# Choice of the experts' tokens rewritten: ranks in 128 partitions, a threshold without bit masks, the list from two sets of one-hot columns, all in one block

## The chip, the core and the metric

The kernel runs on one core of one Trainium2 chip. A core has a matrix engine (TensorE, "PE" in the profile, with "PEld" for its weight loads), three engines for elementwise work (VectorE "DVE", ScalarE "ACT", GpSimd "POOL") and a queue engine (SyncE, "SP") that issues most DMA transfers. The engines run on their own and meet through semaphores. The metric is the device time of one launch in microseconds (us), lower is better.

## What is computed

Eight stages act on `x` of shape (8, 512, 256), that is 4096 tokens of 256 numbers: four cross attentions, and four feed-forward parts between them. The change lies inside one of these, the expert-choice layer. Its reference, cut to what matters here:

```python
scores = jax.nn.sigmoid(h @ gate_w.T)               # h: (4096, 256), 16 experts
cap = math.ceil(T / E * TOP_K)                      # 4096 / 16 * 2 = 512
topk_score, topk_ids = jax.lax.top_k(scores.T, cap) # each expert picks its 512 best tokens
xin = h[topk_ids]
...                                                 # expert MLP on 512 x 256, per expert
flat = (eo * topk_score[..., None]).reshape(-1, Dm)
out = jnp.zeros_like(h).at[topk_ids.reshape(-1)].add(flat)
```

The order within `topk_ids` does not matter for the sum. The kernel needs the 512 token numbers of each of the 16 experts in a tile `index` of 128 partitions x 16 experts x 4, which later indirect DMAs read as lists of rows to fetch and to add to.

## The kernel before, in words

`P` is 128, `S` 512, `CE` 16 (experts), `CAP` 512, `NT` 32 (tiles of 128 tokens), `SB` and `TB` 4. `expert_choice` calls three parts one after the other: `shared_expert` writes the scores of all tokens to `l1f_scoresT` (16 x 4096) in DRAM, `choose_tokens` turns them into `index`, and `run_experts` loads the weights, gathers rows and computes. Between the parts all engines meet at barriers: a `nc.Block()` ends only when every engine is at its end, and `stage_semaphores` clears semaphores and has one more barrier. No weights of the experts are loaded ahead, so nothing of the other two parts lies beside the choice.

`choose_tokens` has five blocks before the change.

1. Set-up. SP loads the scores twice: as `s128` (each expert's row cut in 8 chunks of 512, chunk c of expert e in partition 16 c + e; eight transfers, L2910) and as `s16` (16 partitions x 4096, L2911). GpSimd and VectorE make constants, among them `same`, a 128 x 128 matrix that is 1 where two partitions belong to the same expert.
2. Threshold (L2943 to L2968). The score of rank 512 of each expert is found two bits at a time in 15 rounds of a hardware loop (`Fori`). In a round VectorE forms four candidates from the threshold so far, counts in three passes how many scores reach them (L2950, with a sum along the row), TensorE adds the counts over the 8 chunks of an expert with `same` (two matmuls, L2967 and L2968), and VectorE turns the sums into two bits by masks and exclusive-ors (L2955 to L2960). `chained` gives each dependent instruction a semaphore wait on the one before.
3. Ranks (L2975 to L3006). On `s16`, in 16 partitions of 4096 columns: which scores lie above the threshold, which equal it and still have room, a running count (the scan) as the rank of each chosen token, and from it a slot 0 to 511, with values past 511 for tokens not chosen. TensorE turns this to tokens in partitions (32 transposes, L3006), VectorE cuts the slot in slot / 4 (`slot_p`) and slot modulo 4 (`slot_j`), and makes `numbers`: for each of 4 values of `slot_j`, the token's partition and its tile where it matches, else 0 (L2993 to L2998).
4. List (L3013 to L3029). For each of 32 tiles VectorE builds a one-hot matrix of `slot_p` over 128 values for 16 experts (L3020, 2048 columns), and TensorE multiplies it, expert by expert, with that tile's 8 columns of `numbers` (16 matmuls, L3029), all added up in `psI`.
5. Two instructions make token = 128 x tile + partition and write `index` (L3036, L3038).

The order of everything is as written in the code, engine by engine.

Of the kernel before, what the change touches and what calls it, by code (L numbers as in the profile page):

```python
# [2869 lines left out]
def choose_tokens(nc, A, G, sT_dram, index):  # L2870
# [7 lines left out]
    BITS = 30  # L2878
    with ExitStack() as ctx:
        sb = lambda n, s, d=F32: ctx.enter_context(nc.sbuf_tensor("ch_" + n, s, d))  # L2880
# [3 lines left out]
        same_i, same = sb("same_i", [P, P], I32), sb("same", [P, P])  # L2884
        thr = sb("thr", [P, 1], I32)

        tries, bits, cand, keep = (sb(n, [P, 4], I32) for n in ("tries", "bits", "cand", "keep"))
        count = sb("count", [P, 4])
        s16, above, equal, rank = (sb(n, [CE, N_TOK]) for n in ("s16", "above", "equal", "rank"))
        n_above, room = sb("n_above", [CE, 1]), sb("room", [CE, 1])  # L2890
        slot = sb("slot", [P, NT, CE], I32)
        slot_i = sb("slot_i", [P, NT, CE], I32)
        slot_p, slot_j = sb("slot_p", [P, NT, CE], BF16), sb("slot_j", [P, NT, CE], BF16)
        iota_i, iota_p, iota_j = sb("iota_i", [P, P], I32), sb("iota_p", [P, P], BF16), sb("iota_j", [P, SB], BF16)
        part_i, part_f = sb("part_i", [P, 1], I32), sb("part_f", [P, 1])
        tile_f = sb("tile_f", [P, NT])
        hot_p = sb("hot_p", [P, 2, CE, P], BF16)
        hot_j, numbers = sb("hot_j", [P, NT * CE, SB]), sb("numbers", [P, NT, CE, 2 * SB], BF16)
        zeros = sb("zeros", [P, P], BF16)
        token = sb("token", [P, CE, SB])  # L2900
        psC, psS, psI = psum("psC", [P, S]), psum("psS", [P, NT, CE]), psum("psI", [P, CE, 2 * SB])
        loaded, iotas, set_up, chain = sem("loaded"), sem("iotas"), sem("set_up"), sem("chain")
        counted, summed = sem("counted"), sem("summed")
        slot_ready, slotT_ready, hot_ready, hot_used, index_ready = (sem(n) for n in ("slot_ready", "slotT_ready", "hot_ready", "hot_used", "index_ready"))
# [487 lines left out]
```

## Time and profile before

| | us |
|---|---|
| median of 3 runs | 4851.79 (4846.97 to 4854.86) |
| profiled execution, its own time | 4852.99 |
| span of its trace | 4851.3 |
| TensorE busy in the span | 3982.6 (82%) |
| VectorE busy in the span | 3191.5 (66%) |
| mean granted TensorE clock, as a share of 2.4 GHz | 0.889 |

The span runs from the first to the last instruction of the profiled execution; the rest of its own time lies around it. Busy shares are means over eight very different stages. The view by stretches gives, for each interval of the span, how long each engine was busy and which clock TensorE was granted; the view in order of time lists instructions with start and duration, and in square brackets how long the engine was idle before and what released it. The view by line adds up instructions of one line. A matmul of 4-byte numbers shows as two, since it takes two passes.

### The profile page before, as it was taken

Reading aid. Unit: us, or ns where it says so; the run is one execution under the profiler, and the core shown is the slowest. Engines: PE = TensorE matmul, PEld = TensorE weight load, DVE = VectorE, ACT = ScalarE, POOL = GpSimd, SP = SyncE. Lnnn points to the kernel's source line nnn. Section 1 sums busy time; section 2 is a strip of 40 time slices with the busy share of each in tenths; the row PEclk is TensorE's granted clock in tenths of the full one; section 3 lists DMA queues with packets and bytes.
Section 4 is the critical chain, followed back from the end, with each engine's and each line's share of the span. In section 5 each row is a group of like instructions: output and inputs, shape, how many; then the busy total and the mean of one; then the engine's idle time right before and its main releaser. Section 6 shows DMA issues by size and latency. Waiting matters only on the chain. (4 is left out here: it accounts for less than half of the span.)

```text
span 4851.3 us, 84441 instructions
## 1 busy us (share of the span) xinstructions
PE 3982.6 (82%) x30868; PEld 2871.1 (59%) x30962; DVE 3191.5 (66%) x7093; ACT 2059.9 (42%) x3636; POOL 790.5 (16%) x508
## 2 busy tenths in 40 slices
PE   6599997888467999785389999549997986799899
PEld 5244443777365777674268888425555665355577
DVE  6466664435565666544866666549985885898587
ACT  2255554233112433342034545217775762577611
POOL 4333321301251000000013332310000011100000
PEclk9799998699767999897579999769998998799999
DMA  6333331101220000010034444532210005122100
GB/s 206 108 96 97 99 87 53 64 18 37 94 86 28 17 17 22 27 43 30 0 118 123 129 124 131 164 102 67 67 52 18 1 25 175 57 66 66 38 14 22
DMA packets 202232, 338.12 MB, mean 70 GB/s; under 512 B 25380, under 2 KB 119125, under 8 KB 201910
## 3 DMA queue, kind: packets, MB, share of 16 engines
q1 hardware_dynamic: 186040, 306.81, 19.8%
q0 software_dynamic: 15888, 27.23, 2.7%
q8 instruction: 195, 3.19, 0.3%
q14 instruction: 109, 0.89, 0.1%
HBM read 242.65 MB, written 106.97 MB: 72 GB/s over the span
## 5 line engine op out<-in xcount | busy, mean ns | idle before, releaser
L1900 ACT ACTIVATE a_pT<-a_psS 128x512 f32<-128x512 f32 x1536 | 835.9, 598 | 397.8 <-PE a_psS L1786 392.6
L1972 DVE TENSOR_REDUCE a_mx<-a_psA 128x1 f32<-128x512 f32 x1024 | 656.6, 685 | 82.8 <-PE a_psA L1764 82.8
L1764 PE MATMUL a_psA<-a_ks,a_qs 48*128 48x512 f32 (+1 forms) x1536 | 403.3, 520 | 159.9 <-PEq L46 94.2
L1801 PE MATMUL a_psZ<-a_pT,a_V 128*17 128x128 f32 x12288 | 487.1, 277 | 0.0
L1968 DVE CUSTOM_DVE_ANT_0 a_scored<-a_psA,a_hide_q 128x512 bf16<-128x512 f32 x512 | 332.6, 688 | 190.3 <-PE a_psA L1764 189.2
L1801 PEld LDWEIGHTS a_psZ<-a_pT,a_V 128*17 128x17 f32 x12288 | 272.2, 97 | 270.5 <-issue 160.0
L1764 PEld LDWEIGHTS a_psA<-a_ks,a_qs 48*128 48x128 f32 (+1 forms) x1536 | 150.9, 191 | 405.8 <-issue 174.9
L1786 PE MATMUL a_psS<-a_qs,a_ks 50*128 50x512 f32 (+1 forms) x1536 | 317.4, 406 | 2.7 <-ACT a_pT L1900 0.8
L3264 DVE SCALAR_TENSOR_TENSOR ex_h<-ex_psU,ex_ub,ex_sg 128x512 f32<-128x512 f32 x129 | 96.9, 751 | 188.5 <-PE ex_psU L159 167.5
L1984 POOL TENSOR_TENSOR X<-X,a_osb 128x512 f32<-128x512 f32 x48 | 61.2, 1280 | 938.1 <-ACT a_osb L1887 920.2
L3210 ACT CAST ex_w_h<-X 128x1024 fp32r<-128x1024 f32 x102 | 106.1, 1040 | 231.1 <-DMA X<-in_L_ffn_gw 227.3
L3131 POOL DMA_INDIRECT ex_xg<-l1f_rows,ex_idx_get x72 | 76.4, 1061 | 591.7 <-DVEq L3295 358.6
L3219 ACT ACTIVATE ex_sg<-ex_psG,ex_gb 128x512 f32<-128x512 f32 x129 | 88.8, 688 | 178.6 <-PE ex_psG L159 177.2
L1786 PEld LDWEIGHTS a_psS<-a_qs,a_ks 50*128 50x128 f32 (+1 forms) x1536 | 148.8, 189 | 19.1 <-ACT a_pT L1900 13.1
L1774 PE MATMUL a_psS<-a_hide_k,identb 128*128 128x512 bf16 x418 | 133.8, 383 | 27.7 <-ACT a_pT L1900 15.7
L987 DVE TENSOR_TENSOR m_early_l<-m_ps,m_early_h 128x512 fp32r<-128x512 f32 x70 | 48.4, 692 | 147.5 <-ACT m_early_h L863 147.5
L157 PE MATMUL ex_psY<-ex_w_h,ex_h_h 128*128 128x256 f32 x512 | 144.2, 282 | 0.1
L157 PE MATMUL l1a_psF<-l1a_win_h,l1a_zh 128*128 128x512 f32 x288 | 121.3, 421 | 27.7 <-DVE l1a_zl L2598 14.3
L159 PE MATMUL ex_psY<-ex_w_h,ex_h_l 128*128 128x256 f32 x512 | 143.7, 281 | 0.0
L158 PE MATMUL ex_psY<-ex_w_l,ex_h_h 128*128 128x256 f32 x512 | 143.6, 280 | 0.0
L1144 PE MATMUL p_psY<-p_w,p_h 128*128 128x256 f32 x512 | 132.9, 395 | 12.0 <-ACT p_h L1221 12.0
L1488 POOL TENSOR_TENSOR a_p_cT_l<-a_p_cT,a_p_cT_h 128x1024 fp32r<-128x1024 f32 x24 | 58.0, 2416 | 494.3 <-ACT a_p_cT_h L1455 493.9
(606 smaller groups left out, 10491.9 us busy)
## 6 DMA issues: line engine op xcount, KB each, us to landing
a_k_parts<-a_p_kp SPq DMA_DIRECT2D x96, 256.0 KB
a_q_parts<-a_p_qp SPq DMA_DIRECT2D x96, 256.0 KB
a_qs<-a_q_parts SPq DMA_DIRECT2D x192, 128.0 KB
a_ks<-a_k_parts SPq DMA_DIRECT2D x192, 128.0 KB
X<-in_L_ffn_gw SPq DMA_DIRECT2D x36, 512.0 KB, 3.7
X<-in_L_ffn_up_w SPq DMA_DIRECT2D x36, 512.0 KB, 3.3
X<-in_L_ffn_down_w SPq DMA_DIRECT2D x36, 512.0 KB, 3.9
top_rows<-blank_rows SPq DMA_DIRECT2D x32, 514.0 KB, 11.4
```

Source lines behind the costliest of these rows:

```text
L157: nc.tensor.matmul(out, wh, xh, start=start and n == 0, stop=False, **kw)
L158: nc.tensor.matmul(out, wh, xl, start=False, stop=False, **kw)
L159: last = nc.tensor.matmul(out, wl, xh, start=False, stop=stop and n == len(pairs) - 1, **kw)
L1144: last = nc.tensor.matmul(out, h[:, m % 2, t * P:(t + 1) * P], w2[:, m, :], start=False, stop=(m == MF - 1), skip_group_check=True)
L1764: nc.tensor.matmul(psA[:, unit(a, par) % 3], qs[r, g % ring, p % 2, q * P:(q + 1) * P], ks[r, g % ring, p % 2], start=True, stop=True).the ...
L1774: nc.tensor.matmul(psS[:, unit(t, par) % 3], G.identb[:], hide_k[:, u % 2, kt, :], start=True, stop=False, skip_group_check=True)
L1786: nc.tensor.matmul(psS[:, unit(t, par) % 3], ks[r, g % ring, p % 2, kt * P:(kt + 1) * P], qs[r, g % ring, p % 2], start=(hidden is None), ...
L1801: last = nc.tensor.matmul(psZ[q * VP:q * VP + VW, g % 2, j * P:(j + 1) * P], V[:, b, kt, g % NG * GH + j, :], pT[:, p % 2, par, kt, q * P: ...
L1900: nc.scalar.activation(pT[:, p % 2, par, kt, :], psS[:, unit(t, par) % 3], ACT.Exp).then_inc(exp_done, 1)
L1968: nc.vector.tensor_tensor_reduce(out=scored[:, par], in0=psA[:, unit(a, par) % 3], in1=hide_q[:, b % 2, q, :], scale=1.0, scalar=HIDDEN, o ...
L1972: nc.vector.tensor_reduce(mx[:, p // 2 % 2, par, p % 2, q:q + 1], psA[:, unit(a, par) % 3], AX_X, ALU.max).then_inc(a_used, 1)
L3210: nc.scalar.copy(w_h[:, s, c, :], whole[:, c, :]).then_inc(w_high, 1)
```

## The change

Everything is in `choose_tokens`; the function's interface, `index` and the order of slots in it stay as they were.

- One block in place of five, with no barrier between its parts. `s16` is no longer loaded. SP issues the eight loads, then waits for the end of the work on the tokens.
- Threshold: the 15 rounds are written out in place of a loop. Three candidates, one matmul (L2999 of the changed kernel). Since the number of candidates that are reached, 0 to 3, is just the value of the two bits, VectorE sums the three comparisons (L2952, `passed`), multiplies by the bits' place value and ors that in. The shift of `tries` comes before the wait for TensorE.
- Ranks: on `s128`, 128 partitions x 512 columns. As an expert now lies in 8 partitions, two small products with `same` and `earlier` (1 where a partition has the same expert and an earlier chunk) carry the counts from chunk to chunk (L3001, L3002, L3004). Four 128 x 128 transposes in place of 32 of 16 x 128.
- List: the slot is cut into slot / 16 (32 values, `slot_a`) and slot modulo 16 (16 values, `slot_j`). VectorE writes 16 columns with the token's partition and 16 with its tile (`numbers`, L2979 and L2980, 128 x 512 each) and 32 one-hot columns (`hot_a`, L2982, 128 x 512 each). TensorE takes four experts at a time: 32 values x 4 experts as 128 weight columns and 32 x 4 moving columns, for 32 tiles and 4 groups of experts, 128 matmuls (L3014). Both operands step through SBUF: neighbouring weight columns lie 256 bytes apart, and the moving ones 256 or 1024 bytes. Of the product only the blocks in which both experts are the same are used.
- Tokens: four blocks of 32 partitions each (L2988, L2991), then a transfer to a DRAM tensor `ch_list` and one back that brings them into the layout of `index` (L2911, L2913 of the changed kernel).

The diff, without most of the removed lines, which stand in the listing above; a line that is only "..." marks what is left out:

```diff
@@ -2876,167 +2876,143 @@
+    AW, JW, GROUPED = 32, CAP // 32, 4
     with ExitStack() as ctx:
+        list_dram = nc.dram_tensor("ch_list", [P * CE * SB], I32).ap()
...
+        hot_a, numbers = sb("hot_a", [P, GROUPED, AW, NT * GROUPED], BF16), sb("numbers", [P, 2, JW, NT * CE], BF16)
+        token = sb("token", [P, SB, GROUPED, SB], I32)
+        psC, psS, psI = psum("psC", [P, S]), psum("psS", [P, TB, P]), psum("psI", [P, GROUPED, 2 * JW * GROUPED])
...
                 chunks = sT_dram.rearrange("e (c s) -> c e s", s=S)
                 for c in range(CHUNKS):
                     sp.dma_start(s128[c * CE:(c + 1) * CE, :], chunks[c]).then_inc(loaded, 16)
-                sp.dma_start(s16[:], sT_dram).then_inc(loaded, 16)
-                sp.wait_ge(loaded, 16 * (CHUNKS + 1))
+                sp.wait_ge(token_ready, GROUPED)
+                sp.dma_start(list_dram.rearrange("(p r) -> p r", p=P), token[:].rearrange("p q g j -> p (q g j)")).then_inc(stored, 16)
+                sp.wait_ge(stored, 16)
+                sp.dma_start(index[:].bitcast(I32).rearrange("p (i g) j -> p i (g j)", i=GROUPED),
+                             list_dram.rearrange("(i p r) -> p i r", p=P, i=GROUPED)).then_inc(fetched, 16)
+                sp.wait_ge(fetched, 16)
+                sp.wait_ge(loaded, 16 * CHUNKS)
...
+                nc.gpsimd.iota(offset_i[:], [[-1, P]], base=P, channel_multiplier=1).then_inc(iotas, 1)
+                nc.gpsimd.iota(row_i[:], [[0, 1]], base=0, channel_multiplier=1).then_inc(iotas, 1)
+                nc.gpsimd.iota(tile_i[:], [[0, GROUPED], [1, NT], [0, GROUPED]], base=0, channel_multiplier=0).then_inc(iotas, 1)
...
+                dve.wait_ge(iotas, 4)
                 link(nc.vector.tensor_scalar(same_i[:], same_i[:], CE - 1, None, ALU.bitwise_and))
+                nc.vector.tensor_scalar(ahead[:], offset_i[:], float(P), None, ALU.is_lt)
+                nc.vector.tensor_copy(tile_b[:], tile_i[:])
+                nc.vector.tensor_copy(row_f[:], row_i[:])
                 link(nc.vector.tensor_scalar(same[:], same_i[:], 0.0, None, ALU.is_equal))
+                nc.vector.tensor_tensor(earlier[:], same[:], ahead[:], ALU.mult).then_inc(consts_set, 1)
...
+                dve.wait_ge(consts_set, 1)
+                dve.wait_ge(loaded, 16 * CHUNKS)
+                for i in range(BITS // 2):
+                    if i > 0:
+                        dve.wait_ge(tried, i)
+                    link(nc.vector.tensor_tensor(cand[:], tries[:], thr[:].to_broadcast([P, 3]), ALU.bitwise_or))
                     for n in range(3):
                         last = nc.vector.tensor_scalar(reached[:, n], s128[:], cand[:, n:n + 1].bitcast(F32), 0.0, ALU.is_ge, ALU.add,
                                                        accum_out=count[:, n:n + 1])
                     last.then_inc(counted, 1)
+                    nc.vector.tensor_scalar(tries[:], tries[:], 2, None, ALU.logical_shift_right).then_inc(tried, 1)
                     dve.wait_ge(summed, i + 1)
 
-                    link(nc.vector.scalar_tensor_tensor(keep[:], psC[:, 0:4], float(CAP), bits[:], ALU.is_ge, ALU.mult))
-                    nc.vector.tensor_scalar(bits[:], bits[:], 2, None, ALU.logical_shift_right)
-                    link(nc.vector.tensor_tensor(keep[:, 0:2], keep[:, 0:2], keep[:, 2:4], ALU.bitwise_xor))
-                    link(nc.vector.tensor_tensor(keep[:, 0:1], keep[:, 0:1], keep[:, 1:2], ALU.bitwise_xor))
-                    nc.vector.tensor_tensor(thr[:], thr[:], keep[:, 0:1], ALU.bitwise_or)
-                    link(nc.vector.tensor_scalar(tries[:], tries[:], 2, None, ALU.logical_shift_right))
+                    link(nc.vector.tensor_scalar(reaches[:], psC[:, 0:3], float(CAP), 0.0, ALU.is_ge, ALU.add, accum_out=passed[:]))
+                    link(nc.vector.tensor_scalar(brought[:], passed[:], float(1 << (BITS - 2 - 2 * i)), None, ALU.mult))
+                    link(nc.vector.tensor_tensor(thr[:], thr[:], brought[:], ALU.bitwise_or))
+
+                t = thr[:].bitcast(F32)
+                nc.vector.tensor_scalar(above[:], s128[:], t, 0.0, ALU.is_gt, ALU.add, accum_out=n_above[:])
+                link(nc.vector.tensor_scalar(equal[:], s128[:], t, None, ALU.is_equal))
+                nc.vector.tensor_tensor_scan(rank[:], equal[:], equal[:], 0.0, ALU.add, ALU.max).then_inc(above_counted, 1)
+                dve.wait_ge(room_summed, 1)
+                link(nc.vector.tensor_scalar(room[:], psC[:, 3:4], -1.0, float(CAP), ALU.mult, ALU.add))
+                link(nc.vector.scalar_tensor_tensor(equal[:], rank[:], room[:], equal[:], ALU.is_le, ALU.mult))
+                link(nc.vector.tensor_tensor(above[:], above[:], equal[:], ALU.add))
+                nc.vector.tensor_tensor_scan(rank[:], above[:], above[:], 0.0, ALU.add, ALU.max).then_inc(rank_counted, 1)
+                dve.wait_ge(rank_summed, 1)
+                link(nc.vector.tensor_scalar(shift[:], psC[:, 4:5], 2.0 * CAP, None, ALU.subtract))
+                nc.vector.scalar_tensor_tensor(rank[:], rank[:], shift[:], above[:], ALU.add, ALU.mult).then_inc(slot_ready, 1)
+                dve.wait_ge(slotT_ready, 1)
+                by_tile = slot_i[:].rearrange("p (i c q g) -> p q c i g", i=GROUPED, q=TB, g=GROUPED)
+                for q in range(TB):
+                    last = nc.vector.tensor_scalar(by_tile[:, q], psS[:, q].rearrange("p (c i g) -> p c i g", i=GROUPED, g=GROUPED),
+                                                   2.0 * CAP - 1.0, None, ALU.add)
+                link(last)
+                link(nc.vector.tensor_scalar(part[:], slot_i[:], 4, None, ALU.logical_shift_right))
+                nc.vector.tensor_copy(slot_a[:], part[:])
+                link(nc.vector.tensor_scalar(slot_i[:], slot_i[:], JW - 1, None, ALU.bitwise_and))
+                link(nc.vector.tensor_copy(slot_j[:], slot_i[:]))
+                for j in range(JW):
+                    nc.vector.tensor_scalar(numbers[:, 0, j], slot_j[:], float(j), row_f[:], ALU.is_equal, ALU.mult)
+                    nc.vector.scalar_tensor_tensor(numbers[:, 1, j], slot_j[:], float(j), tile_b[:], ALU.is_equal, ALU.mult)
+                for a in range(AW):
+                    last = nc.vector.tensor_scalar(hot_a[:, :, a], slot_a[:].rearrange("p (i r) -> p i r", i=GROUPED), float(a), None, ALU.is_equal)
+                last.then_inc(hot_ready, 1)
+                dve.wait_ge(list_ready, 1)
+                found = psI[:].rearrange("p g (v q j i) -> p v i q g j", v=2, q=SB, j=SB)
+                rows = [slice(i * AW, (i + 1) * AW) for i in range(GROUPED)]
+                for i in range(GROUPED):
+                    last = nc.vector.tensor_scalar(token[rows[i]], found[rows[i], 1, i], float(P), None, ALU.mult)
+                link(last)
+                for i in range(GROUPED):
+                    nc.vector.tensor_tensor(token[rows[i]], token[rows[i]], found[rows[i], 0, i], ALU.add).then_inc(token_ready, 1)
+                dve.wait_ge(token_ready, GROUPED)
...
+                pe.wait_ge(consts_set, 1)
+                for i in range(BITS // 2):
                     pe.wait_ge(counted, i + 1)
+                    nc.tensor.matmul(psC[:, 0:3], same[:], count[:], start=True, stop=True).then_inc(summed, 1)
+                pe.wait_ge(above_counted, 1)
+                nc.tensor.matmul(psC[:, 3:4], same[:], n_above[:], start=True, stop=False, skip_group_check=True)
+                nc.tensor.matmul(psC[:, 3:4], earlier[:], rank[:, S - 1:S], start=False, stop=True, skip_group_check=True).then_inc(room_summed, 1)
+                pe.wait_ge(rank_counted, 1)
+                nc.tensor.matmul(psC[:, 4:5], earlier[:], rank[:, S - 1:S], start=True, stop=True, skip_group_check=True).then_inc(rank_summed, 1)
                 pe.wait_ge(slot_ready, 1)
+                for q in range(TB):
+                    last = nc.tensor.transpose(psS[:, q], rank[:, q * P:(q + 1) * P], G.ident[:])
                 last.then_inc(slotT_ready, 1)
+                pe.wait_ge(hot_ready, 1)
+                hot = hot_a[:].rearrange("p i a (n g) -> p n g (i a)", g=GROUPED)
+                found = numbers[:].rearrange("p v j (i n g) -> p n g (v j) i", i=GROUPED, g=GROUPED)
+                for g in range(GROUPED):
+                    for n in range(NT):
+                        last = nc.tensor.matmul(psI[:, g], hot[:, n, g], found[:, n, g], start=(n == 0), stop=(n == NT - 1))
+                last.then_inc(list_ready, 1)
```

The order of instructions on VectorE in one threshold round, before (`cand` is the candidates, `psC` the sums, L70 are the register operations of the chained waits inside the loop):

```order
L2948 TENSOR_TENSOR ch_cand<-ch_tries,ch_thr 128x4
L70 ISA
L2950 TENSOR_SCALAR ch_reached,ch_count<-ch_s,ch_cand 128x512 x3
L2953 REGISTER_ALU
L2955 SCALAR_TENSOR_TENSOR ch_keep<-ch_psC,ch_bits 128x4
L70 REGISTER_ALU
L2956 TENSOR_SCALAR ch_bits<-ch_bits 128x4
L2957 TENSOR_TENSOR ch_keep<-ch_keep 128x2
L70 REGISTER_ALU
L2958 TENSOR_TENSOR ch_keep<-ch_keep 128x1
L70 REGISTER_ALU
L2959 TENSOR_TENSOR ch_thr<-ch_thr,ch_keep 128x1
```

and now, from one round's candidates to the next round's:

```order
L2944 TENSOR_TENSOR ch_cand<-ch_tries,ch_thr 128x3
L2946 TENSOR_SCALAR ch_reached,ch_count<-ch_s,ch_cand 128x512 x3
L2949 TENSOR_SCALAR ch_tries<-ch_tries 128x3
L2952 TENSOR_SCALAR ch_reaches,ch_passed<-ch_psC 128x3
L2953 TENSOR_SCALAR ch_brought<-ch_passed 128x1
L2954 TENSOR_TENSOR ch_thr<-ch_thr,ch_brought 128x1
L2944 TENSOR_TENSOR ch_cand<-ch_tries,ch_thr 128x3
```

The shift of `tries` moved ahead of the wait for `psC`, and three instructions stand between `psC` and the next candidates where six did.

TensorE's order from the ranks to the first matmul of the list, before:

```order
L3001 UNCONDITIONAL_BRANCH
L3003 MATMUL ch_psI<-ch_zeros 128x128
L3006 MATMUL ch_psS<-ident,ch_rank 128x16 x32
L2972 UNCONDITIONAL_BRANCH
L3023 UNCONDITIONAL_BRANCH
L3025 UNCONDITIONAL_BRANCH
L3025 ISA
L3029 ISA
L3029 MATMUL ch_psI<-ch_numbers,ch_hot_p 128x8
```

and the whole of its part now:

```order
L2999 MATMUL ch_psC<-ch_count,ch_same 128x3 x15
L3001 MATMUL ch_psC<-ch_n_above,ch_same 128x1
L3002 MATMUL ch_psC<-ch_rank,ch_earlier 128x1
L3004 MATMUL ch_psC<-ch_rank,ch_earlier 128x1
L3007 MATMUL ch_psS<-ident,ch_rank 128x128 x4
L3014 MATMUL ch_psI<-ch_numbers,ch_hot_a 128x128 x128
L2904 UNCONDITIONAL_BRANCH
```

The 512 matmuls with 8 moving columns, in a loop with VectorE's one-hot matrices, have become 128 with 128 moving columns, which start after all columns are made.

SP's queue, from the first loads to the experts' first load (- before, + now):

```order
-L2906 UNCONDITIONAL_BRANCH
-L2910 DMA ch_s<-l1f_scoresT 16x512 x8
-L2911 DMA ch_s<-l1f_scoresT 16x4096
 L2905 UNCONDITIONAL_BRANCH
-L2938 ISA
-L2969 ISA
-L3008 ISA
-L45 ISA x3
+L2909 DMA ch_s<-l1f_scoresT 16x512 x8
+L2911 DMA ch_list<-ch_token 128x64
+L2913 DMA l1f_index<-ch_list 128x4x16
+L2904 UNCONDITIONAL_BRANCH
```

The load of 16 x 4096 is gone, and two transfers that wait for the tokens stand at the end of the choice.

## Rows read from the trace of the kernel before

**Rows 1.** Stretches: start:end, us, busy by engine, PEclk, DMA share, GB/s

```profile
2262.00:2332.00 70.00, 15.18 (x60) 13.89 (x60) 45.37 (x194) 0.00 (x0) 0.00 (x0) 0.50 0.00 0
2332.00:2385.00 53.00, 3.86 (x33) 3.59 (x33) 47.91 (x18) 0.00 (x0) 0.00 (x0) 0.50 0.00 0
2385.00:2464.00 79.00, 66.96 (x512) 53.22 (x512) 72.30 (x34) 0.00 (x0) 0.00 (x0) 0.50 0.00 0
2466.00:3060.00 594.00, 558.04 (x3220) 488.44 (x3220) 355.91 (x507) 279.04 (x377) 186.59 (x136) 0.97 0.49 131
1600.00:2000.00 400.00, 387.68 (x2271) 313.10 (x2270) 274.17 (x849) 157.99 (x342) 0.00 (x0) 1.00 0.05 17
```

**Rows 2.** Order of time, first loads and first round: start us, us, engine, line, op

```profile
2252.79 3.59 SPq L2910 DMA_DIRECT2D ch_s<-l1f_scoresT  x8
2261.66 0.16 DVE L2948 TENSOR_TENSOR ch_cand<-ch_tries,ch_thr 128x4 int32<-128x4 int32 x1 [7.34 <-PEq L2939]
```

**Rows 3.** DMA issues of the first loads: count, size, us to landing

```profile
ch_s<-l1f_scoresT SPq DMA_DIRECT2D x8, 32.0 KB, 1.8
```

**Rows 4.** Order of time, one threshold round

```profile
2271.05 0.16 DVE L2948 TENSOR_TENSOR ch_cand<-ch_tries,ch_thr 128x4 int32<-128x4 int32 x1 [0.39 <-DVE ch_tries L2960]
...
2273.25 0.08 DVE L2950 DVE_READ_ACCUMULATOR ch_reached<-ch_s,ch_cand 128x1 f32 x1
2273.39 0.59 PE L2967 MATMUL ch_psC<-ch_count,ch_same 128*128 128x3 f32 x2 [3.66 <-DVE ch_reached L2950]
2273.84 0.57 PE L2968 MATMUL ch_psC<-ch_count,ch_same 128*128 128x1 f32 x2
2274.44 0.16 DVE L2955 SCALAR_TENSOR_TENSOR ch_keep<-ch_psC,ch_bits 128x4 int32<-128x4 f32 x1 [1.11 <-PE ch_psC L2968]
...
2274.91 0.16 DVE L2958 TENSOR_TENSOR ch_keep<-ch_keep 128x1 int32<-128x1 int32 x1
2275.10 0.16 DVE L2959 TENSOR_TENSOR ch_thr<-ch_thr,ch_keep 128x1 int32<-128x1 int32 x1
...
2275.73 0.16 DVE L2948 TENSOR_TENSOR ch_cand<-ch_tries,ch_thr 128x4 int32<-128x4 int32 x1 [0.39 <-DVE ch_tries L2960]
```

**Rows 5.** Order of time, from threshold to columns

```profile
2332.26 4.47 DVE L2977 TENSOR_SCALAR_CACHE_REDUCE ch_above<-ch_s,ch_thr 16x4096 f32<-16x4096 f32 x1 [0.84 <-PEq L2970]
...
2339.21 8.68 DVE L2980 TENSOR_TENSOR_SCAN ch_rank<-ch_equal 16x4096 f32<-16x4096 f32 x1
...
2365.59 4.41 DVE L2985 SCALAR_TENSOR_TENSOR ch_rank<-ch_rank,ch_above 16x4096 f32<-16x4096 f32 x1
...
2376.01 0.69 DVE L2988 CAST ch_slot_i<-ch_psS 128x512 int32<-128x512 f32 x1 [3.69 <-PE ch_psS L3006]
...
2377.19 0.43 DVE L2990 CAST ch_slot_p<-ch_slot 128x512 bf16<-128x512 int32 x1
...
2378.45 2.29 DVE L2993 TENSOR_TENSOR ch_hot_j<-ch_slot_j,ch_iota_j 128x2048 f32<-128x2048 bf16 x1
2380.78 1.29 DVE L2997 TENSOR_SCALAR ch_numbers<-ch_hot_j,ch_part_f 128x2048 bf16<-128x2048 f32 x1
```

**Rows 6.** Order of time, the experts' 128x128 transposes

```profile
2479.30 1.97 PE L3164 MATMUL ex_psT<-ident,ex_xg 128*128 128x128 f32 x8 [16.04 <-DMA ex_xg<-l1f_rows,ex_idx_get]
```

**Rows 7.** Groups by line in the choice: busy us, mean ns, idle before

```profile
L3020 DVE TENSOR_TENSOR ch_hot_p<-ch_slot_p,ch_iota_p 128x2048 bf16<-128x2048 bf16 x32 | 71.9, 2289 | 4.8 <-PE ch_psI L3029 3.0 <-DVEq L3015 1.7
...
L2950 DVE TENSOR_SCALAR_CACHE_REDUCE ch_reached<-ch_s,ch_cand 128x512 bf16<-128x512 f32 x45 | 31.2, 744 | 0.5
```

**Rows 8.** Order of time, first and last of the list, then tokens

```profile
2385.96 4.49 DVE L3020 TENSOR_TENSOR ch_hot_p<-ch_slot_p,ch_iota_p 128x2048 bf16<-128x2048 bf16 x2 [1.69 <-DVEq L3015]
...
2461.16 2.01 PEld L3029 LDWEIGHTS ch_psI<-ch_numbers,ch_hot_p 128*128 128x128 bf16 x16 [0.20 <-issue]
2463.60 0.23 DVE L3036 TENSOR_SCALAR ch_token<-ch_psI 128x64 f32<-128x64 f32 x1 [2.58 <-PEq L3012]
2463.86 0.22 DVE L3038 TENSOR_TENSOR l1f_index<-ch_token,ch_psI 128x64 uint32<-128x64 f32 x1
```

More of the change, by code:

```diff
@@ L2883, in choose_tokens @@
         s128, reached = sb("s128", [P, S]), sb("reached", [P, 3, S], BF16)
[L2884 to L2904, printed above, removed]
+        same_i, same, earlier = sb("same_i", [P, P], I32), sb("same", [P, P]), sb("earlier", [P, P])
@@ new lines, in choose_tokens @@
+        offset_i, ahead = sb("offset_i", [P, P], I32), sb("ahead", [P, P])
+        thr, tries, cand, brought = sb("thr", [P, 1], I32), sb("tries", [P, 3], I32), sb("cand", [P, 3], I32), sb("brought", [P, 1], I32)
+        count, reaches, passed = sb("count", [P, 3]), sb("reaches", [P, 3]), sb("passed", [P, 1])
+        above, equal, rank, n_above = sb("above", [P, S]), sb("equal", [P, S]), sb("rank", [P, S]), sb("n_above", [P, 1])
+        room, shift = sb("room", [P, 1]), sb("shift", [P, 1])
@@ new lines, in choose_tokens @@
+        psC, psS, psI = psum("psC", [P, S]), psum("psS", [P, TB, P]), psum("psI", [P, GROUPED, 2 * JW * GROUPED])
+        loaded, iotas, chain, stored, fetched = sem("loaded"), sem("iotas"), sem("chain"), sem("stored"), sem("fetched")
+        consts_set, counted, summed, tried = sem("consts_set"), sem("counted"), sem("summed"), sem("tried")
+        above_counted, room_summed, rank_counted, rank_summed, slot_ready, slotT_ready, hot_ready, list_ready, token_ready = (
+            sem(n) for n in ("above_counted", "room_summed", "rank_counted", "rank_summed", "slot_ready", "slotT_ready", "hot_ready",
+                             "list_ready", "token_ready"))
@@ L2962, in _ @@
+                link(last)
+                for i in range(GROUPED):
+                    nc.vector.tensor_tensor(token[rows[i]], token[rows[i]], found[rows[i], 0, i], ALU.add).then_inc(token_ready, 1)
+                dve.wait_ge(token_ready, GROUPED)
             @block.tensor
             def _(pe):
-                with pe.Fori(0, BITS // 2) as i:
+                pe.wait_ge(consts_set, 1)
+                for i in range(BITS // 2):
                     pe.wait_ge(counted, i + 1)
-                    nc.tensor.matmul(psC[:, 0:3], same[:], count[:, 0:3], start=True, stop=True)
-                    nc.tensor.matmul(psC[:, 3:4], same[:], count[:, 2:3], start=True, stop=True).then_inc(summed, 1)
@@ L3033, in choose_tokens @@
-        with nc.Block() as block:
-            @block.vector
-            def _(dve):
-                nc.vector.tensor_scalar(token[:], psI[:, :, SB:], float(P), None, ALU.mult).then_inc(index_ready, 1)
-                dve.wait_ge(index_ready, 1)
-                nc.vector.tensor_tensor(index[:], token[:], psI[:, :, 0:SB], ALU.add).then_inc(index_ready, 1)
-                dve.wait_ge(index_ready, 2)
+                pe.wait_ge(hot_ready, 1)
+                hot = hot_a[:].rearrange("p i a (n g) -> p n g (i a)", g=GROUPED)
```

82 lines of the change are left out of this document (6 added, 76 removed).

## The prediction

> **What bounds the kernel now.** I read the stretches first, to see whether anything lies beside the choice of tokens. The choice fills 2252.8 to 2464.1 us. In its three stretches ACT and POOL are busy for 0.00 us and no DMA moves a byte [rows 1]; the PE and VectorE alternate. So each microsecond that leaves the chain of VectorE, PE and VectorE again leaves the kernel, and each one added to it counts in full. The granted clock there is 0.50, so PE works at 1.2 GHz, even in the list, where it is busy for 66.96 of 79 us [rows 1]. Then I went through the choice in order of time, to price its parts from one start to the next: start of the first round at 2261.66 [rows 2], threshold to 2332.26, ranks to 2376.01, cutting of slots to 2378.45, columns to 2385.96 [rows 5, 8], list to 2463.60, tokens to 2464.08 [rows 8]. The list and the ranks are over half. The list is bound by VectorE: 32 one-hot matrices at 2289 ns are 71.9 us [rows 7].
>
> **The change, part by part.** VectorE starts a dependent small instruction 0.19 us after the one before (2274.91 to 2275.10 [rows 4]). A long one costs a fixed 0.15 us and 1.04 ns for each column: 4.41 us for 4096 columns [rows 5]. The next one, if independent, starts before it has ended: the counting passes last 0.744 [rows 7] and start 0.67 apart, three in the 2.01 us from 2271.24 (candidates and 0.19) to 2273.25 [rows 4], so 0.08 is taken off.
>
> 1. Start. The eighth load is issued by 2256.38 and its issue began about 0.4 us earlier; loads land 1.8 us after issue [rows 2, 3], so at 2257.8. The first round can start at 2258.0 in place of 2261.66, when a larger load and a barrier had been waited for. Gain 3.6. The new constants on VectorE and GpSimd lie beside these loads and cost nothing; without that cover the 512-column cast would cost 0.43 [rows 5] and the rest less than 1.
>
> 2. Threshold. A round takes 2271.05 to 2275.73, 4.68 us [rows 4]; with the loop's entry and the barrier behind it 15 rounds take 2332.26 - 2261.66 = 70.6. In a new round 2.34 us go from the candidates to PE's start (2273.39 - 2271.05), one matmul takes 0.59 (the second began 0.45 later and is gone), the way back 0.03; then the summed comparison 0.25 (0.16 and a read of the sum, 0.08), place value 0.19, or 0.19. That is 3.59, and the shift of `tries` lies beside the matmul. 15 x 3.59 = 53.9, a gain of 16.7. Bounds: 3.4 (the read of the sum costs nothing) to 3.9 (it and the added semaphore cost 0.3 more), so 12 to 20.
>
> 3. Ranks. Before 2376.01 - 2332.26 = 43.75. With 512 columns: above 0.75 with the read of its sum, equal 0.46 (as the cast of 512 at two columns a cycle, 0.43, with its wait [rows 5]), scan 0.15 + 8.53/8 = 1.22, two small matmuls 1.14 (2273.39 to 2274.44 and the hand-over [rows 4]), room 0.19, two passes of 0.71, scan 1.25, one matmul 0.65, shift 0.19, one pass 0.71. That is 7.98. Four transposes: eight such took 1.97 at the start of the experts [rows 6], so 4 x 0.25 and 0.2 around them, 1.2. Sum 9.2, a gain of 34.5. Bounds 33 to 36.
>
> 4. Cutting the slots. Before 2.44 (2376.01 to 2378.45). One read of PSUM of 0.69 becomes four of 128 columns, starts 0.21 apart, so 0.95; the rest stays. Cost 0.3.
>
> 5. Columns. Before 7.51 (2378.45 to 2385.96), with a barrier of 1.69 [rows 8]. Now 48 compares of a 2-byte tile with a constant (16 L2979, 32 L2982) and 16 two-operand ones (L2980), all of 512 columns. No row has a compare from 2 bytes to 2 bytes. The nearest is the cast of 4 to 2 bytes, 0.43, two columns a cycle (as the 2048 columns of L2997 in 1.29); the slowest form is 0.69, one a cycle; below lies the 0.16 of a 4-column one [rows 4, 5]. I take the nearest, 0.35 from start to start. A two-operand pass over three reads ran at one column a cycle (L2985, and 2-byte ones too, L3020 [rows 7]), so 0.61. 48 x 0.35 + 16 x 0.61 = 26.6, a cost of 19.1. Bounds: 48 x 0.16 + 16 x 0.35 = 13.3 to 64 x 0.61 = 39.0, so 6 to 31. Nothing hides them, since PE waits for the last.
>
> 6. List. Before 77.64 (2385.96 to 2463.60). Now 128 matmuls with nothing between them. 16 weight loads took 2.01 us [rows 8], 0.13 for each, at the clock of 0.50, and 128 columns fit in that time at 1.2 GHz. 128 x 0.13 and 0.3 to fill and hand over are 17.1, a gain of 60.5. Bounds: at the full clock, which PE has elsewhere (1.00 in 1600 to 2000 [rows 1]), half of it, 8.4; and if each took as long as a two-pass transpose (1.97/8 = 0.25 [rows 6]), 31.8. So 46 to 69.
>
> 7. Tokens. Before 0.48. Now eight instructions over 64 columns; one took 0.22 [rows 8]; 0.14 apart and one wait, 1.2. Cost 0.7.
>
> 8. To DRAM and back. No such pair is in the choice before. Two transfers of 32 KB, as each of the first loads, at 1.8 us to landing [rows 3], and 0.3 for each hand-over: cost 4.2. Bounds: 3.6, and twice as much (8.4), as they move pieces of 256 and 64 bytes. SP has nothing queued behind them until the experts' loads, which waited for the end of the choice before too.
>
> Sum: -3.6 - 16.7 - 34.5 + 0.3 + 19.1 - 60.5 + 0.7 + 4.2 = -91.0. From the profiled execution's own 4852.99 that gives 4762.0; from the median, 1.2 lower, 4760.8. What follows the choice starts as before, and PE comes to it after some 8 us of rest, cold as before. Prediction: 4761.
>
> **What a page says of the list's reads.** The row for PE's loads [rows 8] is for columns that lie side by side. The new weight columns lie 256 bytes apart, and no row has that; I took the row. The Trainium skill, "SBUF — State Buffer", section "Specifications (TRN2)", says that SBUF has lines of 16 bytes and wants at least two hits on a line for full bandwidth, and that each step to a new line pays a penalty. It has no figure for it. By that rule, which speaks against this change, the list would go to the upper bound or past it.
>
> **Rivals.**
>
> A. The columns are faster: a 2-byte tile moves four columns a cycle. Then a compare is 0.15 + 0.13 = 0.28 and its start to start 0.20, 48 x 0.15 = 7.2 less: 4754. For it: two columns a cycle were had even with 4-byte operands (L2990, L2997 [rows 5]). Against it: no row shows more than two, and L3020's 2-byte compare made one [rows 7]. The Trainium skill, "VectorE: DVE Perf Modes", section "The perf-mode tier table", gives a bf16 `tensor_scalar` in SBUF four elements a cycle. This is the case it speaks of, and no run here shows it yet.
>
> B. The list is slower: strided operands hold PE at 0.25 us a matmul: 32 in place of 17, 4776. For it: every operand read steps over lines. Against it: nothing in the trace, which has no such read.
>
> C. The rounds do not get shorter: written-out code comes no faster than the loop, or the wait for `tried` and the summed comparison cost what they save. The sum without its 16.7: 4778. Against it: three dependent instructions less and a matmul less are in the chain that the timeline shows closed, with 0.39 us of loop besides [rows 4].
>
> D. Slower than before, through the clock. The choice is now 211 us in which PE is at 0.50 or idle, and the experts behind it have 0.97 with 558 us of busy PE [rows 1]. If that clock is paid for by the rest before it, a shorter rest could cost it. To take back 91 us, 558 must become 649, a mean clock of 0.97 x 558/649 = 0.83; below that the kernel is slower than before. At 0.80 it would be 558 x 0.97/0.80 - 558 = 119 longer: 4880. Against it: 1600 to 2000 has 1.00 over 400 us with PE busy for 387.68 [rows 1], so long work does not wear the clock down here.
>
> **From this to the numbers.** Forecast (4761) 0.43, A 0.32, B 0.15, C 0.07, D 0.01, and 0.02 for something unforeseen in the change's disfavour. Its bounds all together reach from -3.6 - 20 - 36 + 6 - 69 + 4 = about -118 (4735) to -3 - 12 - 33 + 31 - 46 + 9 = -54 (4799), but they will hardly fall on one side together. The 8 in 10 go from 4743 (A, and the list at the faster clock for part of its length) to 4780 (B, C, or the columns at one a cycle). A measurement of this kernel can tell 0.2%, some 10 us, from no change. Every case but D and part of the last lies 70 us or more below: faster 0.98, same 0.01, slower 0.01.
>
> **What would show it.** First round at 2258; rounds of 3.6 us; ranks to the first cut of slots in 9 us; L2979 and L2982 at 0.43 each (A: 0.28) and L2980 at 0.69; the list's matmuls 0.13 us apart (B: 0.25), with a clock above 0.50 if its dense work raises it; 4 us from the last token to the end of the second transfer; the choice some 120 us long in place of 211, and the experts' 594 us unchanged (D: longer, at a lower clock). It is wrong if the choice takes over 150 us, or if the experts change by more than 5.

## The result and the profile after

The changed kernel takes 4771.12 us (median of 4 runs, 4767.6 to 4783.91) and the kernel before took 4849.38 beside it (median of 4). The ratio is 0.9837, with a 95% interval of 0.982 to 0.9853, so 71 to 87 us less. A later set on another occasion gave 0.9841 (0.9827 to 0.9854). The time came out 10 us above the forecast of 4761, and inside the range of 4743 to 4780.

First the stretches of the changed kernel, in the columns of [rows 1]: the rounds, the ranks and slots, then the list and the experts.

```profile
2256.00:2306.00 50.00, 8.23 (x28) 7.02 (x28) 39.62 (x171) 0.00 (x0) 0.00 (x0) 0.50 0.00 0
2306.00:2318.00 12.00, 2.71 (x10) 2.14 (x10) 8.66 (x20) 0.00 (x0) 0.00 (x0) 0.50 0.00 1
...
2339.00:2372.00 33.00, 33.00 (x128) 27.63 (x127) 0.00 (x0) 0.00 (x0) 0.00 (x0) 0.50 0.00 0
2379.00:2973.00 594.00, 558.11 (x3220) 489.32 (x3220) 355.18 (x507) 279.04 (x377) 184.16 (x136) 0.97 0.49 130
```

The experts' row is that of before to 0.07 us of PE and to the same 0.97. The list has turned round: VectorE was its engine before, and now PE is busy for all 33 us of the row with nothing beside it, still at 0.50. Next the timeline, from the loads to the second round's candidates:

```profile
2247.89 3.59 SPq L2909 DMA_DIRECT2D ch_s<-l1f_scoresT  x8
...
2248.38 1.61 POOL L2923 IOTA ch_tile_i<- 128x512 int32 x1
...
2252.93 0.16 DVE L2944 TENSOR_TENSOR ch_cand<-ch_tries,ch_thr 128x3 int32<-128x3 int32 x1 [1.56 <-DMA ch_s<-l1f_scoresT]
...
2255.96 0.16 DVE L2952 TENSOR_SCALAR_CACHE_REDUCE ch_reaches<-ch_psC 128x3 f32<-128x3 f32 x1 [0.66 <-PE ch_psC L2999]
...
2256.55 0.16 DVE L2944 TENSOR_TENSOR ch_cand<-ch_tries,ch_thr 128x3 int32<-128x3 int32 x1
```

VectorE waits for the last load, as it should, and no longer for a barrier [rows 2]. From 2256.55 the next round starts at 2260.10, 3.55 later; it was 4.68 [rows 4]. The rest, in the same view:

```profile
2306.29 0.75 DVE L2957 TENSOR_SCALAR_CACHE_REDUCE ch_above<-ch_s,ch_thr 128x512 f32<-128x512 f32 x1
...
2314.42 1.12 PE L3007 MATMUL ch_psS<-ident,ch_rank 128*128 128x128 f32 x4 [1.04 <-DVE ch_rank L2967]
2315.57 0.88 DVE L2971 TENSOR_SCALAR ch_slot_i<-ch_psS 128x128 int32<-128x128 f32 x4 [1.21 <-PE ch_psS L3007]
...
2318.21 0.35 DVE L2979 TENSOR_SCALAR ch_numbers<-ch_slot_j,ch_row_f 128x512 bf16<-128x512 bf16 x1
2318.48 0.69 DVE L2980 SCALAR_TENSOR_TENSOR ch_numbers<-ch_slot_j,ch_tile_b 128x512 bf16<-128x512 bf16 x1
2319.08 0.35 DVE L2979 TENSOR_SCALAR ch_numbers<-ch_slot_j,ch_row_f 128x512 bf16<-128x512 bf16 x1
...
2338.67 33.48 PE L3014 MATMUL ch_psI<-ch_numbers,ch_hot_a 128*128 128x128 bf16 x128 [23.14 <-DVE ch_hot_a L2982]
2372.19 0.92 DVE L2988 TENSOR_SCALAR ch_token<-ch_psI 32x64 int32<-32x64 f32 x4 [33.58 <-PE ch_psI L3014]
...
2374.14 0.35 SPq L2911 DMA_DIRECT2D ch_list<-ch_token  x1
2375.63 0.38 SPq L2913 DMA_DIRECT2D l1f_index<-ch_list  x1
2378.59 0.34 SPq L82 DMA_DIRECT2D ex_ub<-in_L_ffn_up_b  x1
```

The parts, from the start of one to the start of the next, against the prediction's:

| part | before | after | change | predicted |
|---|---|---|---|---|
| 1 start | 8.87 | 5.04 | -3.8 | -3.6 |
| 2 threshold | 70.60 | 53.36 | -17.2 | -16.7 |
| 3 ranks | 43.75 | 9.28 | -34.5 | -34.5 |
| 4 cutting | 2.44 | 2.64 | +0.2 | +0.3 |
| 5 columns | 7.51 | 20.46 | +13.0 | +19.1 |
| 6 list | 77.64 | 33.52 | -44.1 | -60.5 |
| 7 tokens | 0.48 | 1.95 | +1.5 | +0.7 |
| 8 DRAM and back | 1.23 | 4.45 | +3.2 | +4.2 |
| sum | 212.5 | 130.7 | -81.8 | -91.0 |

The profiled spans differ by 85.5 (4851.3 and 4765.8). The choice gives 81.8 of it; what runs before the choice, unchanged, was 4.9 shorter in this execution, and what follows 1.2 longer. That first part alone moves a single time by more than 10 us: the loads of the choice begin at 2247.89 here, at 2258.14 in e7, the same kernel, and at 2265.27 in e6, where everything ahead of the choice is unchanged too. So the experiments below are read from the lengths of parts inside the choice. The groups of the two parts that missed show the cause's place (busy us and mean ns):

```profile
L3014 PEld LDWEIGHTS ch_psI<-ch_numbers,ch_hot_a 128*128 128x128 bf16 x128 | 28.0, 220 | 28.6 <-DVE ch_hot_a L2982 23.5
...
L2982 DVE TENSOR_SCALAR ch_hot_a<-ch_slot_a 128x512 bf16<-128x512 bf16 x32 | 6.6, 292 | 0.0
```

A weight load takes 220 ns, against 2.01/16 = 126 in [rows 8], and the matmuls come 33.48/128 = 0.262 apart. A compare takes 0.29, and the 32 start 6.6/32 = 0.205 apart. The row of the weight loads alone would put the list's cost down to the weights; the experiments say otherwise.

### The profile page after: what moved, and what is told of

It reads as the page before. It is cut to its first block and busy times, and to the rows that moved or that the text cites. A ratio compares the mean times of both kernels' runs of the same rounds, so it can differ in the third digit from the quotient of the medians.

```text
span 4765.8 us, 82796 instructions
## 1 busy us (share of the span) xinstructions
PE 3944.8 (83%) x30525; PEld 2829.8 (59%) x30525; DVE 3097.5 (65%) x7110; ACT 2060.2 (43%) x3636; POOL 789.5 (17%) x509
## 5 line engine op out<-in xcount | busy, mean ns | idle before, releaser
L1774 PE MATMUL a_psS<-a_hide_k,identb 128*128 128x512 bf16 x512 | 155.1, 385 | 16.5 <-ACT a_pT L1900 2.9
```

Source lines behind the costliest of these rows:

```text
L1774: nc.tensor.matmul(psS[:, unit(t, par) % 3], G.identb[:], hide_k[:, u % 2, kt, :], start=True, stop=False, skip_group_check=True)
```

## The experiments

**Where the list's 16 us went.** Two kernels, e1 and e2, have four more batches of 128 matmuls behind the list, with results that nothing uses. They differ in the order of the batches alone, so that what belongs to the operands and what to the clock can be told apart. The edit, shortened (`dense_x` takes 128 neighbouring columns of `numbers`, as `dense_w` does of `hot_a`; the loops are left out):

```
+ dense_w = lambda m: flat_a[:, m * P:(m + 1) * P]
+ four = numbers[:].rearrange("p v j (m i) -> p m (v j) i", i=GROUPED)
+ matmul(psX[:, 1], dense_w(m), found[:, n, g])    # moving stepped
+ matmul(psX[:, 2], hot[:, n, g], four[:, m])      # weights stepped, moving in runs of four
+ matmul(psX[:, 3], hot[:, n, g], dense_x(m))      # weights stepped
+ matmul(psX[:, 4], dense_w(m), dense_x(m))        # both dense
```

> The changed kernel with four extra batches of 128 bf16 matmuls of 128 x 128 behind its list, into a PSUM tile that nothing reads: dense weight columns with stepped moving ones, stepped weights with moving columns in runs of four, stepped weights with dense moving ones, both dense. VectorE does 20 extra instructions on spare tiles while PE works on the list. The list's own matmuls are 0.262 us apart. Theory W (stepped weight columns set the pace): about 0.13 in the first batch, 0.26 in the second and third, 0.13 in the fourth. Theory M (stepped moving columns set it): 0.26, 0.13, 0.13, 0.13. Theory S (steps do not matter, a weight load and 128 moving columns at 1.2 GHz stand behind one another): 0.26 in all four. In W and M the clock may rise to 1.00 in dense batches, then 0.07. VectorE: a compare with two constants 0.29, with a pointer operand 0.35, a 2-byte product of two tiles 0.43 to 0.69, writes in runs of four 0.29 if runs are enough, writes to every fourth element 0.69. Time: after + 60 to 135 us.

> The same four batches in the reverse order (both dense first, dense weights with stepped moving columns last). If a batch's pace comes from its operands and the clock level, each keeps it; if it comes from the clock that the batches before brought, the paces go with the place instead: W and M then differ from e1 by up to a factor of two in the batches behind the dense one.

PE's timeline behind the list in the first (L3034 moving stepped, L3037 weights stepped with runs of four, L3040 weights stepped, L3043 both dense), and then in the reversed kernel (there L3034 is both dense, L3037 weights stepped, L3040 weights stepped with runs of four, L3043 moving stepped):

```profile
2376.01 28.00 PE L3034 MATMUL ch_psX<-ch_numbers,ch_hot_a 128*128 128x128 bf16 x128
2403.83 16.80 PE L3037 MATMUL ch_psX<-ch_numbers,ch_hot_a 128*128 128x128 bf16 x128
2420.46 14.77 PE L3040 MATMUL ch_psX<-ch_numbers,ch_hot_a 128*128 128x128 bf16 x128
2435.07 7.31 PE L3043 MATMUL ch_psX<-ch_numbers,ch_hot_a 128*128 128x128 bf16 x128
```

```profile
2381.41 9.80 PE L3034 MATMUL ch_psX<-ch_numbers,ch_hot_a 128*128 128x128 bf16 x128
2391.04 14.86 PE L3037 MATMUL ch_psX<-ch_numbers,ch_hot_a 128*128 128x128 bf16 x128
2405.73 16.81 PE L3040 MATMUL ch_psX<-ch_numbers,ch_hot_a 128*128 128x128 bf16 x128
2422.38 27.98 PE L3043 MATMUL ch_psX<-ch_numbers,ch_hot_a 128*128 128x128 bf16 x128
```

Each batch keeps its length wherever it stands, but for the dense one, which has part of its time at 0.50 in the reversed order. Stepped moving columns alone cost 0.22 a matmul, stepped weights alone 0.115 (0.13 with the moving columns in runs of four), both together 0.262, neither 0.056. Of the three theories in the expectation M is the nearest: W wanted 0.26 wherever the weights are stepped, S in all four batches. M had the first batch somewhat too slow (0.26). The pace comes from the operands, as rival B says, and not from the clock: the reversed kernel's dense batch began at 0.50, and had 35 matmuls in its first 3.6 us, 0.10 each (columns as in [rows 1]).

```profile
2381.40:2385.00 3.60, 3.60 (x35) 3.59 (x34) 1.75 (x8) 0.00 (x0) 0.00 (x0) 0.50 0.04 9
```

The times, one execution each, are 4826.83 for e1, some 4 us under what was expected, and 4840.32 for e2.

**Which operand, in the real list.** In e5 `numbers` alone is stored so that a matmul's moving columns lie 8 bytes apart, in e6 `hot_a` alone, so that its weight columns do. Of each edit only the shape of the tile is shown; the views that write and read it follow.

```
 e5: -numbers [P, 2, JW, NT * CE]             +numbers [P, NT, 2, JW, CE]
 e6: -hot_a   [P, GROUPED, AW, NT * GROUPED]  +hot_a   [P, NT, GROUPED, AW, GROUPED]
```

> The change with `numbers`, the moving operand, stored so that its 128 columns lie 8 bytes apart; the weights from `hot_a` keep their 256-byte step. Theory M (the moving operand's steps are what costs; the earlier batches gave 0.22 us a matmul with stepped moving columns and dense weights, 0.115 to 0.13 with stepped weights and moving columns in runs): 128 matmuls in 15 to 17 us, 0.12 to 0.13 each, nearly all of the 18 us that storing both gained; the clock rises above 0.50 inside the list. Rival W (both operands' steps add, each with its own share): about 0.115 + 0.12 apart, so 20 to 25 us. One product without its partner kept slow, R (whichever operand is stepped holds the pair at 0.26): 33 us.

> The change with `hot_a`, the weights, stored so that their 128 columns lie 8 bytes apart; the moving operand keeps its steps of 256 and 1024 bytes. Theory M: 0.22 us a matmul, 28 us, as with fully dense weights, so 5 us gained of the 18; the clock stays at 0.50. Rival W: near 0.15 to 0.20 each, 20 to 25 us. R: 33 us.

The list's line in e5, then in e6 (duration in ns: minimum, median, maximum; first and last start):

```profile
L3015 PE MATMUL ch_psI<-ch_numbers,ch_hot_a x128: 296/309/411, 2347.4 to 2363.7; 128*128 128x128 bf16 x128
```

```profile
L3014 PE MATMUL ch_psI<-ch_numbers,ch_hot_a x128: 388/397/401, 2356.1 to 2383.9; 128*128 128x128 bf16 x128
```

From the first start to the last, over 127, that is 0.128 a matmul with the moving operand packed and 0.219 with the weights packed. So the list takes 16.6 us in e5 and 28.1 in e6, as theory M says, and the moving operand carries nearly all of the cost; W (20 to 25 us in both) and R (33 in both) fall. The clock rose above 0.50 in e5's list (0.86 over all of it) and stayed at 0.50 in e6's. The weight loads of e5 still last 213 ns each, with starts 0.128 apart, so a long load in the profile is not yet a slow list. The single times, 4768.08 and 4782.69, are one execution each; they lie within the spread of the changed kernel's own and say nothing beside the lists.

**Both packed.** e3 has both edits; e8 is the same kernel once more, beside the changed kernel (e7) on the same chip.

> The changed kernel with the columns stored so that neighbouring weight columns and neighbouring moving columns lie 8 bytes apart (four groups of experts side by side), in place of 256 and 1024; the same 128 matmuls, 64 columns and tokens. Theory of lines (steps over 16-byte lines set the pace, two hits on a line are enough): matmuls 0.13 apart, list 17 us in place of 33.5, 4771 - 16.5 = 4754; 4746 if the clock rises. Theory S: list stays 33.5, 4771. VectorE may lose: if runs of four or sixteen elements drop a compare from 0.29 to 0.43 or 0.69, the columns cost 48 x 0.14 to 0.40 = 7 to 19 more, and the time stays at 4761 to 4773.

> The changed kernel once more, beside the version with both operands packed on the same chip, so that their distance can be read without the spread between chips: 4765 to 4775.

> Both operands of the list at 8-byte steps, again. If the list's steps are what made the sum of the prediction come out short, this run is 17 to 19 us under the changed kernel beside it, near 4752; if the gain of the first run was spread between chips, it is within 5 of it.

The list in e3, then in e7 and in e8:

```profile
2341.07 15.31 PE L3015 MATMUL ch_psI<-ch_numbers,ch_hot_a 128*128 128x128 bf16 x128 [23.13 <-DVE ch_hot_a L2983]
2356.41 0.92 DVE L2989 TENSOR_SCALAR ch_token<-ch_psI 32x64 int32<-32x64 f32 x4 [15.40 <-PE ch_psI L3015]
```

```profile
2349.07 33.46 PE L3014 MATMUL ch_psI<-ch_numbers,ch_hot_a 128*128 128x128 bf16 x128 [23.13 <-DVE ch_hot_a L2982]
```

```profile
2345.15 15.38 PE L3015 MATMUL ch_psI<-ch_numbers,ch_hot_a 128*128 128x128 bf16 x128 [23.13 <-DVE ch_hot_a L2983]
```

It takes 15.3 in place of 33.5, and the columns 20.5 as in the changed kernel (2320.61 to 2341.07): writing `hot_a` in runs of four elements and `numbers` in runs of sixteen costs VectorE nothing, though the expectation allowed it 7 to 19 us. e3 took 4752.21 (4749.33 to 4755.1), ratio to before 0.9794 (0.9764 to 0.9823). In the second set e7 took 4774.1 (4765.49 to 4780.64) and e8 4757.68 (4749.62 to 4773.24): 16 less at the median, with ratios to before of 0.9841 (0.9827 to 0.9854) and 0.9821 (0.9801 to 0.984). Those two intervals overlap, and two of e8's five runs lie among e7's, so the times alone leave the gain open, though the medians are near the 17 to 19 that was expected and not within 5. What shows the gain is the list itself, 18 us shorter in both pairs of profiles.

**At which step the cost begins.** e9 has, behind the packed list, batches of 64 matmuls that differ in one step alone (the edit, shortened to loops).

```
+ step = lambda t, m, s: t[:, m % 32:m % 32 + P * s:s]
+ for s in (1, 2, 4, 8, 16, 32, 64, 127):          # bf16 elements
+     matmul(psX, step(flat_a, m, 1), step(flat_n, m, s))   # 64 times each
+ for s in (8, 64, 127):
+     matmul(psX, step(flat_a, m, s), step(flat_n, m, 1))
```

> The packed version and behind its list eleven batches of 64 matmuls of 128 bf16 columns whose results are not used, in this order: dense weights with the moving columns 2, 4, 8, 16, 32, 64, 128 and 254 bytes apart, then dense moving columns with the weights 16, 128 and 254 bytes apart. Theory L (a read of SBUF costs by the line of 16 bytes that it touches): moving columns up to 8 bytes apart cost as dense ones (0.055 at the full clock), from 16 bytes on 0.22 and no more after that. Rival G (the cost grows with the step all the way, through banks or rows of the memory): a staircase, 0.06 at 8 bytes, about 0.1 at 32, 0.22 only at 254. Weights: L gives 0.115 for all three steps, G a rise from 0.06 to 0.115. The whole takes 704 matmuls, some 80 to 110 us more than the packed version: 4830 to 4865.

PE's timeline, in the order 2, 4, 8, 16, 32, 64, 128, 254 bytes between moving columns, then 16, 128, 254 between weights:

```profile
2357.63 3.78 PE L3020 MATMUL ch_psX<-ch_numbers,ch_hot_a 128*128 128x128 bf16 x64
2361.25 3.96 PE L3022 MATMUL ch_psX<-ch_numbers,ch_hot_a 128*128 128x128 bf16 x64
2365.05 7.66 PE L3024 MATMUL ch_psX<-ch_numbers,ch_hot_a 128*128 128x128 bf16 x64
2372.53 14.77 PE L3026 MATMUL ch_psX<-ch_numbers,ch_hot_a 128*128 128x128 bf16 x64
2387.12 15.09 PE L3028 MATMUL ch_psX<-ch_numbers,ch_hot_a 128*128 128x128 bf16 x64
2402.03 14.05 PE L3030 MATMUL ch_psX<-ch_numbers,ch_hot_a 128*128 128x128 bf16 x64
2415.90 14.07 PE L3032 MATMUL ch_psX<-ch_numbers,ch_hot_a 128*128 128x128 bf16 x64
2429.80 14.53 PE L3034 MATMUL ch_psX<-ch_numbers,ch_hot_a 128*128 128x128 bf16 x64
2444.15 6.30 PE L3036 MATMUL ch_psX<-ch_numbers,ch_hot_a 128*128 128x128 bf16 x64
2450.28 5.96 PE L3038 MATMUL ch_psX<-ch_numbers,ch_hot_a 128*128 128x128 bf16 x64
2456.08 3.98 PE L3040 MATMUL ch_psX<-ch_numbers,ch_hot_a 128*128 128x128 bf16 x64
```

All of it took 4842.9, inside the expected 4830 to 4865. From start to start and over 64, moving columns cost 0.057, 0.059, 0.117, 0.228, 0.233, 0.217, 0.217 and 0.224. The cost doubles from 4 to 8 and again from 8 to 16 bytes, and stays from there on. The clock does not explain the step to 0.228, though it was 0.50 for most of the batches from 16 bytes on: over the first 2 us of the batch at 16 bytes it was still 0.92, and its first 11 matmuls came 0.23 apart, as all 64 did. So L had the end right, that nothing counts after 16 bytes, and was wrong in that 8 bytes are not free; G's staircase up to 254 is refuted. The original 256 and 1024 bytes are simply past the last step. The Trainium skill, "SBUF — State Buffer", section "Specifications (TRN2)", asks for two hits on a line of 16 bytes for full bandwidth. At the full clock two hits (8 bytes) gave half the pace of dense columns here, and four (4 bytes) all of it; the measurement decides. At 0.50 the two differ little, 0.12 in the first 3 us of e3's list against 0.10. The weights fit neither theory: 0.091 at 128 bytes, 0.060 at 254, both at 1.00, and 0.115 at 256 in e1. The 0.096 at 16 bytes had a mean clock of 0.57 and so does not tell its step from the clock, as dense operands too took 0.10 at 0.50. Why weights are cheap at 254 stays open.

**The threshold alone.** e4 is the kernel before with the new rounds, in its old block with its old ranks and list.

> The kernel before with only its threshold changed: rounds written out, three candidates, one matmul, the sum of comparisons in place of masks. Nothing else. By the parts: -15 x (4.68 - 3.56) - 0.3 = -17, so 4832. If the rounds gained by something else of the change (no barrier, one block), less than half of that: 4841 to 4849.

From the first candidates to `above`:

```profile
2259.18 0.16 DVE L2949 TENSOR_TENSOR ch_cand<-ch_tries,ch_thr 128x3 int32<-128x3 int32 x1 [7.33 <-PEq L2939]
...
2262.73 0.16 DVE L2949 TENSOR_TENSOR ch_cand<-ch_tries,ch_thr 128x3 int32<-128x3 int32 x1
...
2313.53 4.47 DVE L2973 TENSOR_SCALAR_CACHE_REDUCE ch_above<-ch_s,ch_thr 16x4096 f32<-16x4096 f32 x1 [0.89 <-PEq L2966]
```

That is 54.35 in place of 70.6, 16.3 less, with rounds of 3.55: rival C falls, and the saving needs none of the other parts. The time is 4829.89 (8 runs, 4821.59 to 4854.6) against 4853.69, ratio 0.9965 (0.9941 to 0.9989), that is 5 to 29 less, which holds the 16.

**Compares on VectorE.** e1 also had twenty dummy passes behind the columns. They ran beside the list's matmuls, where each lasted longer than the 0.29 of a compare with PE idle, so they bound the prices without setting them:

```profile
2342.59 1.18 DVE L2987 TENSOR_SCALAR ch_spare<-ch_slot_j 128x512 bf16<-128x512 bf16 x4
2343.69 1.20 DVE L2989 TENSOR_SCALAR ch_spare<-ch_slot_j,ch_row_f 128x512 bf16<-128x512 bf16 x4
2344.71 2.26 DVE L2991 TENSOR_TENSOR ch_spare<-ch_slot_j,ch_tile_b 128x512 bf16<-128x512 bf16 x4
2346.78 1.13 DVE L2993 TENSOR_SCALAR ch_by_four<-ch_slot_a 128x512 bf16<-128x512 bf16 x4
2347.81 4.19 DVE L2995 TENSOR_SCALAR ch_by_one<-ch_slot_a 128x512 bf16<-128x512 bf16 x4
```

A compare and product with two constants (L2987) and one compare with a per-partition value (L2989) start 0.28 and 0.26 apart, so the 0.27 of L2979 could not be put down to either. Products of two 2-byte tiles (L2991) start 0.52 apart, nearer to the 0.60 of L2980 than to a compare. Writes in runs of four elements (L2993) cost no more than the compares beside them, 0.26; writes to every fourth element alone (L2995) start 1.05 apart, four times as much.

## Why the prediction was right, and where it was not

The bound was read rightly: the choice stood alone, every microsecond of its chain counted, and the experts moved by less than 0.1 us of PE. D falls with that. The choice is 130.7 us long, not over 150.

Steps 1 to 4 came out within 0.6 us each. All of them were sums of durations from rows of the same operations on other sizes. For step 2 the round was put at 3.59 and is 3.55, for step 3 9.2 and 9.28. The constants did hide, but they are more than was priced (0.43 and less than 1): the new IOTA alone takes 1.61 us. It ends at 2250.0, and VectorE still waits 1.56 for the loads. Of step 3, the four transposes took 1.12, 0.28 each. They are of 4-byte numbers and show as four records, one each (L3007), while a product like L2999 shows as two; so the name "two-pass transpose", which the upper bound of step 6 uses for the 0.25 of [rows 6], rests on nothing in the trace.

Step 6 failed. "128 x 0.13" took the price of a load of weights that lie side by side for one whose columns lie 256 bytes apart, and took the moving side as free; a matmul is 0.262. List 33.5 in place of 17.1, 16.4 in the change's disfavour, 1.7 past the upper bound of 31.8, which rival B took as its price. That B's 0.25 lies so near to 0.262 is luck: it is the time of a transpose of 4-byte numbers, another operation. The decisive operand was not the one that the step looked at: packing the weights alone leaves 0.219, packing the moving columns alone 0.128. The prediction named the rule on lines and set it at 0.15 for want of a row. What the runs add is the size. With steps of 8 bytes the step's 0.13 would have been right, for another reason: such matmuls take 0.12 at 0.50 as at 1.00, while wholly dense ones take 0.10 at 0.50 and 0.06 at 1.00.

Step 5 was mis-sized the other way. Rival A holds in full for the 32 compares of L2982: one lasts 0.29 and is 0.205 from the next, where 0.43 and 0.35 were taken from a 4-byte cast. The 16 of L2979 lie between A and the forecast, 0.35 long, with the next start 0.27 later; L2980's is 0.60 later, as predicted (0.61). 32 x 0.205 + 16 x 0.27 + 16 x 0.60 = 20.5 in place of 26.6, 6.1 in its favour. With four columns in 1.04 ns, 512 columns and the fixed 0.15 make 0.28. The Trainium skill, "VectorE: DVE Perf Modes", section "The perf-mode tier table", had those four a cycle for a bf16 `tensor_scalar`. The 0.29 of L2982 agrees; the 0.35 of L2979, a `tensor_scalar` too, does not quite.

A and B were given as rivals, each alone. Both happened, and their errors partly cancel: +16.4 - 6.1, with +0.8 for the tokens, -1.0 for the transfers and -0.9 in steps 1 to 4, are +9.2, the difference of -81.8 from -91.0. That the time came within 10 of the forecast is owed in part to this luck: the case that the forecast stood for, 0.43 of the chances, was not the true one. The range did not need the luck, since the misses of step 6 or of step 5 alone (4777, 4755) lie in it. The 10 itself is not measured finely: four runs of the kernel spread over 16 us.

The two small steps: the eight instructions of step 7 start 0.24 apart and not 0.14. Step 8 took 4.45 in all, near its 4.2, but 1.23 stood there before, between the last token and the experts' first load, and the step took nothing off for it. Its pieces of 256 and 64 bytes cost nothing that a transfer of 32 KB did not: landing after 1.5 and 1.8.

## What to carry to other kernels

Before pricing a matmul by a row, look at how far apart the columns of both operands lie in SBUF. Here a matmul with 128 moving bf16 columns took 0.06 us with steps up to 4 bytes and 0.12 with 8, at the full clock, and 0.22 from 16 bytes on at either level of the clock. The order of the axes in two scratch tiles was worth 18 us. Choose as the innermost axis one that leaves the moving columns of a matmul at most 8 bytes apart, better 4, even if VectorE then writes only short runs: runs of four elements cost it nothing, single elements with gaps four times as much.
